# Four GpSimd subtractions make the low halves of the normalised x, and the norms yield 2048 times the normalised value

## The reference

```
x  = x + attention(layernorm(x), ctx)     # x: 16 x 512 x 256, ctx: 16 x 64 x 256, float32
x  = x + ffn(layernorm(x))
layernorm(v) = (v - mean(v)) / sqrt(var(v) + 1e-5)       # over the last axis
attention: q, k, v are projected by Wq, Wk, Wv and then to one head of 16;
           softmax(q.k / 4, masked), times v, the head repeated 16 times, times Wo
ffn: h = gelu(x @ (alpha1 * sign(w1))^T + b1)            # 1024 hidden
     out = h @ (alpha2 * sign(w2))^T + b2
```

## Time and profile before

| engine | busy us | share of the span | instructions |
|---|---|---|---|
| TensorE, products | 309.1 | 81% | 2087 |
| VectorE | 286.4 | 75% | 637 |
| ScalarE | 261.4 | 69% | 334 |
| GpSimd | 237.6 | 63% | 412 |

### The profile page before, as it was taken

One profiled execution on the slowest core, in us unless ns is written; L12 is line 12 of the kernel. 1 busy time (PEld: TensorE's weight loads), 2 busy tenths in 40 slices (PEclk: granted clock), 3 DMA queues, 4 the chain that ended last, 5 costly groups with the idle time before them and its releaser, 6 DMA issues.

```text
span 379.5 us, 6245 instructions
## 1 busy us (share of the span) xinstructions
PE 309.1 (81%) x2087; PEld 206.6 (54%) x2087; DVE 286.4 (75%) x637; ACT 261.4 (69%) x334; POOL 237.6 (63%) x412
## 2 busy tenths in 40 slices
PE   5867714466989898979898989897979799999994
PEld 3533612323656565657565656565656565766664
DVE  1782357378798989897898889885989798886554
ACT  1155532057979796959796969794879788896780
POOL 1213023748659795967688868896588865847521
PEclk9975675568999999989999999998999999999999
DMA  8920022535637674756566756675375736331402
GB/s 260 383 98 3 0 56 61 119 103 111 173 66 200 104 213 68 205 97 191 87 182 111 205 87 177 115 194 100 92 187 134 171 93 139 89 71 56 113 0 111
DMA packets 83263, 47.67 MB, mean 126 GB/s; under 512 B 73496, under 2 KB 76704, under 8 KB 83232
## 3 DMA queue, kind: packets, MB, share of 16 engines
q1 hardware_dynamic: 82320, 47.24, 50.3%
q10 hardware_dynamic: 912, 0.05, 0.2%
HBM read 21.19 MB, written 8.39 MB: 78 GB/s over the span
## 4 chain that ended last, share of the span: by engine, by line
PE 36%; DVE 25%; DMA 22%; issue 9%; ACT 3%; SPq 2%; POOL 1%; DVEq 0%; POOLq 0%
PE psZ L1352 13%; DMA xT_hi<-ctxT 12%; PE psY L1337 9%; DMA x_in<-in_x 9%; DVE x L817 5%; DVE h_lo L826 4%; PE psW L1295 3%; DVE w_sb L733 3%; DVE w_sb L840 3%; DVE st_raw L703 3%; PE psW L1210 2%; PE psW L1316 2%; ACT V_hl L583 1%; SPq L296 1%; SPq L302 1%
## 5 line engine op out<-in xcount | busy, mean ns | idle before, releaser
L1352 PE MATMUL psZ<-sgn2T,h_hi 128*128 128x256 f16 x512 | 117.1, 276 | 0.0
L1352 PE MATMUL psZ<-sgn2T,h_lo 128*128 128x256 f16 x512 | 116.9, 275 | 0.0
L569 ACT ACTIVATE psY<-psY,b_col,alpha1x 128x512 f32<-128x512 f32 x128 | 93.2, 748 | 27.7 <-PE psY L1337 25.6
L1337 PE MATMUL psY<-xT_hi,sgn1T 128*128 128x512 f16 x256 | 99.0, 387 | 8.3 <-DVE h_lo L826 8.1
L1337 PE MATMUL psY<-xT_lo,sgn1T 128*128 128x512 f16 x256 | 98.5, 385 | 0.0
L826 DVE SCALAR_TENSOR_TENSOR h_lo<-psY,h_scale,h_hi 128x1024 f16<-128x1024 f32 x64 | 81.0, 1266 | 16.1 <-ACT h_hi L578 16.0
L481 POOL TENSOR_TENSOR w_sb<-w_sb,x1b 128x256 f32<-128x256 f32 x62 | 43.1, 727 | 57.3 <-DVE w_sb L840 57.3
L578 ACT ACTIVATE h_hi<-psY,h_scale 128x1024 f16<-128x1024 f32 x64 | 71.3, 1114 | 5.9 <-ACT psY L569 0.4
L1352 PEld LDWEIGHTS psZ<-sgn2T,h_hi 128*128 128x128 f16 x512 | 50.6, 99 | 10.8 <-issue 1.9
L1352 PEld LDWEIGHTS psZ<-sgn2T,h_lo 128*128 128x128 f16 x512 | 50.7, 99 | 9.2
L470 POOL TENSOR_TENSOR x1b<-x,b_bc 128x256 f32<-128x256 f32 x64 | 54.3, 881 | 0.3
(11 more groups left out here) (150 smaller groups left out, 439.8 us busy)
## 6 DMA issues: line engine op xcount, KB each, us to landing
x_in<-in_x SPq DMA_DIRECT2D x16, 512.0 KB, 5.6
ctx_sb<-in_x SPq DMA_DIRECT2D x16, 512.0 KB, 4.4
out_x<-w_sb SPq DMA_DIRECT2D x15, 512.0 KB, 3.0
w_sb<-in_L_ffn_w SPq DMA_DIRECT2D x2, 1024.0 KB, 9.1
ctx_sb<-in_ctx SPq DMA_DIRECT2D x1, 1024.0 KB, 6.8
out_x<-w_sb SPq DMA_DIRECT2D x2, 256.0 KB, 2.1
wk_sb<-in_L_xattn_Wk SPq DMA_DIRECT2D x1, 256.0 KB, 3.3
wq_sb<-in_L_xattn_Wq SPq DMA_DIRECT2D x1, 256.0 KB, 3.6
```

The source lines that it names most:

```text
L569: nc.scalar.activation(y, y, ACT.Gelu, bias=b1_col[:, c:c + 1], scale=alpha1x[:, c:c + 1]).then_inc(gelu_done, 1)
L1337: last = nc.tensor.matmul(psY[q % 2][:, c % 2, :], sgn1T[:, k, c * P:(c + 1) * P], part[b % 2][:, :, k, :], start=(n == 0), stop=(n == 2 * ...
L1352: last = nc.tensor.matmul(Z[n][:, (j % 2) * D:(j % 2 + 1) * D], part[q][:, u, j * P:(j + 1) * P], sgn2T[:, 2 * q + u, :], start=(q == 0 an ...
```

## The change

GpSimd gets a function split_x(b) for the x-hat of the input (n = 0), batches 1 to 15. It waits for the high halves of ScalarE and for the transpose that read the buffer before, and subtracts in four instructions of 256 columns. It stands in GpSimd's order behind shift(0) for batch 1, behind shift(1) for batch 2, and in step(b) between norm(b+1, 1) and norm(b+4, 0) for batch b+3. VectorE's calls for n = 0 go away, but for batch 0.

The norms of both n make 2048 times the value: the variance plus eps is multiplied by 2048^-2 before the power of -0.5. So ScalarE's Copy has no scale, and the subtractions are plain ones: VectorE's for n = 1 and for batch 0 become tensor_tensor.

```diff
 def norm(b, n):
-    nc.gpsimd.tensor_scalar(vare[n][:, :], st[n][b % 2][:, :, 1], 1.0, EPS, ALU.mult, ALU.add) \
+    nc.gpsimd.tensor_scalar(vare[n][:, :], st[n][b % 2][:, :, 1], X_SCALE ** -2,
+                            EPS * X_SCALE ** -2, ALU.mult, ALU.add) \
         .then_inc(norm_steps[n], 1)
...
+def split_x(b):                                  # GpSimd
+    if absent(b) or b == 0:
+        return
+    wait(pool, lo_turned[0], 16 * (b - 2))
+    pool.wait_ge(xh_hi_done[0], val(b, 1, 1) - 1)
+    for j in range(T):
+        last = nc.gpsimd.tensor_tensor(xh_lo[0][b % 2][:, j, :], xh[0][b % 2][:, j, :],
+                                       xh_hi[0][b % 2][:, j, :], ALU.subtract)
+    last.then_inc(xh_split[0], 1)
...
 shift(0)
+split_x(1)
 norm(2, 0)
 shift(1)
+split_x(2)
...
 def step(b):                                     # GpSimd
     norm(b + 1, 1)
+    split_x(b + 3)
     norm(b + 4, 0)
...
-nc.scalar.activation(xh_hi[n][b % 2], xh[n][b % 2][:, :, :], ACT.Copy,
-                     scale=X_SCALE).then_inc(xh_hi_done[n], 1)
+nc.scalar.activation(xh_hi[n][b % 2], xh[n][b % 2][:, :, :], ACT.Copy) \
+    .then_inc(xh_hi_done[n], 1)
...
-nc.vector.scalar_tensor_tensor(out=xh_lo[n][b % 2], in0=xh[n][b % 2][:, :, :],
-                               scalar=X_SCALE, in1=xh_hi[n][b % 2], op0=ALU.mult,
-                               op1=ALU.subtract).then_inc(xh_split[n], 1)
+nc.vector.tensor_tensor(xh_lo[n][b % 2], xh[n][b % 2][:, :, :], xh_hi[n][b % 2],
+                        ALU.subtract).then_inc(xh_split[n], 1)
...
-split_x(1, 0)                                    # VectorE, start-up
...
-split_x(2, 0)
...
 def step(b):                                     # VectorE
     raw_statistics(b + 1, 1)
-    split_x(b + 3, 0)
     statistics(b + 1, 1)
```

More of the change, by code:

```diff
@@ L517, in copy_turned @@
                     nc.scalar.activation(xT_hi[n][0][:, :, k, :],
-                                         (W, Z)[n][k].rearrange("p (j t) -> p j t", j=T), ACT.Copy,
-                                         scale=X_SCALE).then_inc(pe_turned_hi[n], 1)
+                                         (W, Z)[n][k].rearrange("p (j t) -> p j t", j=T), ACT.Copy) \
+                        .then_inc(pe_turned_hi[n], 1)
             def round_x(b, n):
@@ L718, in split_turned @@
                     dve.wait_ge(pe_turned_hi[n], m + 1)
[L719 to L722, removed]
+                    nc.vector.tensor_tensor(
+                        xT_lo[n][0][:, :, k, :], (W, Z)[n][k].rearrange("p (j t) -> p j t", j=T),
+                        xT_hi[n][0][:, :, k, :], ALU.subtract).then_inc(pe_turned_lo[n], 1)
             def split_x(b, n):
```

## The result

The changed kernel takes 469.1 us (median of 4 runs, 467.72 to 470.05) against 383.82 us of the kernel before in the same set: a ratio of 1.222, 95% interval 1.2174 to 1.2266. It is 85 us slower. The forecast was 462 us in a range of 438 to 488. The profiled execution took 468.7 us, its span is 466.9 us, and the mean granted TensorE clock is 0.82 in place of 0.919. Lines of the kernel have moved: the score product is L1306, the shift L470, x1+b2 L483, the residual add L494, the norm's last instruction L447, GpSimd's subtraction L460.

What follows compares the result with a forecast made beforehand. It took a loop through split, low halves' transpose and score product as the bound, now lengthened by GpSimd's queue order. Turns 69.4, start-up 7.1 and end 1.6 gave +78 us: 462 us, range 438 to 488.

Steps and rivals of the forecast that it cites:

- What bounds the kernel, and the order in GpSimd's queue: Loop through split, low halves' transpose and score product, 19.2 us a turn; GpSimd's split would start at 221.0, not end at 215.86.
- the signs it named: Score product waits of 6 us or more, transpose landing in 3.1 us, turns alternating 23 to 27 us, clock at 0.50.
- Scale folded in: 0: Scale as an immediate in the norm: 0 us; VectorE's splits as tensor_tensor taken at 1.2 us.
- Four subtractions: 3.0 us: GpSimd's split in the new loop: 2.8 us from the two-input f32 add, plus 0.2 for meeting split_e.
- x1+b2 back to 2.79 us: GpSimd's four adds, 3.78 us beside VectorE's split, take 2.79 without it: 1.0 us back each turn.
- End of the split to the score product: 3.2 us: Transpose of the low halves in the new loop, without the loads that stretched it to 4.7 us.
- The turns: New loop through GpSimd: 23.6 us without values, 26.4 with; six of each 300.0 against 230.6 us, +69.4 us.
- just in time: x1's statistics ready for GpSimd's norm about 13 us after the score product starts.
- The clock, as a sum: Half clock after TensorE's longer stops: 6 x 0.3 + 6 x 1.6 + 1.6 = 13 us.
- the clock holds: TensorE keeps full clock through the stops before the score products: 13 us less, 449 us; chance 0.13.
- Ends: Start-up puts batch 3's score product at 95.6 instead of 88.45, +7.1 us; behind the last one half clock adds +1.6 us.
- Rivals: Dearer operations 473 to 488 us (0.15); partly taken up 400 to 436 (0.08); GpSimd load 384 (0.02); faster 364 (0.02).

Runs made afterwards that it cites:

- the last experiment: Kernel before with load_x and load_res moved behind the transposes, plus VectorE's split_x(b+3, 0) moved ahead of the statistics of x1: 375.78 us, ratio 0.974.
- the idle products: Changed kernel, plus 26 idle TensorE products of 512 columns ahead of each score product from batch 4 on: 447.25 us, ratio 1.1656.
- the scale alone: Kernel before with norms of 2048 times the value and plain subtractions, all on VectorE in the old order: 384.23 us, ratio 0.9936.
- the early load: Kernel before with load_x(b+5) issued behind turn_e(b+2), in place of load_x(b+4) ahead of the transposes of batch b+3: 366.2 us, ratio 0.952.

## Why the prediction was right

- **What bounds the kernel, and the order in GpSimd's queue.** Right, and the signs it named came: stops of 6.3 to 8.3 us in front of the score products, a transpose of the low halves that lands in 3.3 us (median), turns that alternate, and half clock at each such product. The four places in the queue give 388.7, 392.2, 469.1 and 531.6 us with the same instructions. From the changed place on, each norm in front costs its full length in each turn. Ahead of it there is slack: the place behind the shift is only 3.5 us better than the one behind x1+b2. In the turn looked at (221 to 227 us) the low halves' transpose took 4.2 us there, right behind the high halves', in place of 3.1, and in five turns GpSimd waited 0.9 to 1.8 us for ScalarE's high halves.
- **Scale folded in: 0.** Right, and VectorE's fifteen tensor_tensor of 1024 columns took 1.21 to 1.22 us, as taken. So the 1.26 us of L847 for 512 columns isn't the instruction's own price; it has GpSimd's last adds beside it, and takes 1.26 us in the changed kernel too.
- **Four subtractions: 3.0 us.** They took 2.74, so the term was 0.26 us too large, 3 us in twelve turns. Where split_e isn't beside them, in the kernels with an earlier or a later place, they take 2.55 us: the row for two f32 inputs was 0.25 us too long for one f32 and one f16. The 0.2 us for the meeting with split_e came as taken: in the changed kernel's turns one of the four took up to 0.86 us in place of 0.67.
- **x1+b2 back to 2.79 us.** Right (2.78), with no split of VectorE beside it any more. By the Trainium skill (SBUF — State Buffer, section "SBUF: two separate sides") the two engines exclude each other there for a whole instruction. The trace agrees: 3.78 us with the split beside the adds, 2.78 without. In the last experiment VectorE pays instead, 3.0 us, which is more than one instruction of GpSimd.
- **End of the split to the score product: 3.2 us.** It took 3.4.
- **The turns.** 23.6 and 26.4 us were forecast; 23.4 and 28.0 (means of six each) came. The term that was too small is the turn with values: score product to residual add took 10.2 instead of 9.8 us, and 1.1 us of GpSimd's wait for x1's statistics, which I had called "just in time", were not in the sum. The first hangs on TensorE at half clock: with the idle products it is 8.2 us in all six turns. The second does in part: with them the wait is gone in three of the six turns and still 1.1 to 1.4 us in the other three. I had taken 3.3 us of half clock after a stop; it was 4.3 us in the turn shown. The twelve turns came to 308.6 us, where 300.0 were forecast.
- **The clock, as a sum.** I priced it at 13 us; filling TensorE's stops gave 22 us. The difference is about what the forecast lacks, 7 us of the time (462 to 469) and 9 us of the profiled span. The rival "the clock holds" didn't happen, but its number (449 us) is close to the 447 us of the kernel in which the idle products mostly hold the clock.
- **Ends.** The score product of batch 3 came at 96.49 us; 95.6 was forecast.
- **Rivals.** With the subtractions behind the shift, GpSimd in VectorE's place costs 5 us with the old loads and 7 us with the early one. At the changed place GpSimd isn't short of time, since it waits 119.6 us for VectorE's w_sb; the subtractions count there as a length on the loop. VectorE's relief bought nothing in any kernel: 388.7 against 384.2 us, and 373.0 against 366.2 us, are both losses.

Left open: how the 5 us between the scale alone and the subtractions behind the shift (old loads) divide between GpSimd's load and its waits for ScalarE; whether the start of the first turns, where the clock is low in every kernel, could be filled too; how the 18 us of the early load divide; and what decides whether VectorE's split waits for one GpSimd add or for the whole row. None of these was tried.

## What to carry to other kernels

Before work is moved to an engine with idle time, find the place in its queue, read off what stands ahead of it there, and follow the result to whoever waits for it; idle time behind that place is worth nothing, and once the slack of the result is used up, each microsecond ahead of it is paid in every turn of the loop. Where the new turn makes TensorE stand still for longer, price the clock from a row where that happened, and also for what it does to the waits that were just in time. And look at the DMAs issued right ahead of the one that is waited for: one load moved by a few lines was worth 18 us here, while the change relieved VectorE of 18.9 us of work (286.4 to 267.5) and gained nothing by it.

## What the runs showed of the hardware that wasn't expected

- Idle products on TensorE made a kernel faster by 22 us of 469, since the mean granted clock stayed at 0.91 to 0.925 in place of 0.82.
- When VectorE's two-input split starts while GpSimd runs two-input instructions back to back, it can go either way. In the last experiment it waited for the shift and all four adds, in four turns (4.2 to 4.3 us in place of 1.21), and the adds kept their 2.79 us. In the kernel before it also started in the middle of the row, 1.5 us in, took 1.72 us, and the adds were stretched from 2.79 to 3.78 us.
- The clock fell at about 271.1, 3.7 us after TensorE had stopped at 267.4, while it stood, so that a product starting at 273.70 found it low from its first column.
